# Masks of attention tiles: two of a group's sixteen on GpSimd, one on VectorE, thirteen on TensorE

## The reference, cut to what matters

```python
q, k, v = (proj(Wq), proj(Wk), proj(Wv))              # 8 sequences, 16 heads, 512 tokens, 16 features
scores = jnp.einsum('bhsd,bhtd->bhst', q, k) * scale
scores = jnp.where(mask[None, None, :, :], -jnp.inf, scores)
attn = jax.nn.softmax(scores, axis=-1)
out = jnp.einsum('bhst,bhtd->bhsd', attn, v)
```

## Time and profile before

| | |
|---|---|
| median of three runs | 1219.8 us (1218.94 to 1219.91) |
| the profiled execution: its time | 1216.96 us |
| the profiled execution: its span | 1215.2 us |
| TensorE busy | 1139.1 us (94%) |
| VectorE busy | 824.7 us (68%) |
| ScalarE busy | 736.8 us (61%) |
| GpSimd busy | 534.0 us (44%) |
| mean granted TensorE clock | 0.983 of 2.4 GHz |

### The profile page before, as it was taken

The page is one execution under the profiler, slowest core; times in us unless marked ns, Lnnn a source line. Parts: engine busy times, 40 slices in busy tenths (PEclk is TensorE's granted clock), DMA queues, the critical chain, the costliest instruction groups (busy, mean ns, idle before and its releaser), DMA issues.

```text
span 1215.2 us, 23411 instructions
## 1 busy us (share of the span) xinstructions
PE 1139.1 (94%) x7533; PEld 769.8 (63%) x7590; DVE 824.7 (68%) x2331; ACT 736.8 (61%) x1632; POOL 534.0 (44%) x805
## 2 busy tenths in 40 slices
PE   6899999999989989998888899999999999999978
PEld 3333433434434334343322899999999999999968
DVE  4688879687897887877772444464555655667647
ACT  2266666575666666666546566566666666666645
POOL 7234225484673765747535347546222222323210
PEclk9899999999999999999889899999999999999999
DMA  6654635647448455483543658975655774833536
GB/s 194 185 192 153 200 114 178 200 166 196 136 162 258 140 165 159 153 251 104 177 173 118 228 152 283 340 220 114 189 152 133 233 233 121 277 61 67 157 87 208
DMA packets 101456, 213.52 MB, mean 176 GB/s; under 512 B 10885, under 2 KB 71181, under 8 KB 92886
## 3 DMA queue, kind: packets, MB, share of 16 engines
q1 hardware_dynamic: 87030, 193.34, 49.3%
q0 software_dynamic: 14304, 18.69, 8.3%
HBM read 239.15 MB, written 74.29 MB: 258 GB/s over the span
## 4 chain that ended last, share of the span: by engine, by line
PE 67%; POOL 11%; issue 5%; DVE 5%; DMA 4%; ACT 3%; SPq 3%; another core or an unknown queue 0%; DVEq 0%; POOLq 0%; ACTq 0%
PE bank L1023 36%; PE bank L1123 6%; PE bank L1092 5%; PE bank L1104 5%; PE bank L1108 4%; POOL routed L1882 3%; DMA w_parts<-in_W 2%; PE bank L1068 2%; PE bank L1141 2%; DVE junk L1551 1%; ACT pt L1284 1%; POOL ssq L793 1%; SPq L879 1%; PE bank L1181 1%; PE bank L1076 1%
## 5 line engine op out<-in xcount | busy, mean ns | idle before, releaser
L1284 ACT ACTIVATE pt<-bank 128x512 f32<-128x512 f32 x512 | 300.5, 595 | 178.2 <-PE bank L1108 125.2
L1551 DVE CUSTOM_DVE_ANT_0 junk<-bank,mneg 128x512 bf16<-128x512 f32 x512 | 336.1, 684 | 100.5 <-PE bank L1092 99.5
L1023 PE MATMUL bank<-hid,w 128*128 128x256 f32 x1872 | 241.9, 286 | 4.2 <-DVE hid L1699 4.2
L1699 DVE TENSOR_TENSOR hid<-full,hid 128x256 fp32r<-128x256 f32 x312 | 138.4, 449 | 148.0 <-ACT full L1358 145.8
L1892 POOL DMA_INDIRECT x<-yout,rows x78 | 122.6, 1572 | 263.8 <-ACT yout L1363 235.5
L1023 PEld LDWEIGHTS bank<-hid,w 128*128 128x128 f32 x1872 | 228.6, 191 | 5.2 <-issue 3.1
L1353 ACT ACTIVATE hid<-bank,biases 128x256 fp32r<-128x256 f32 x312 | 150.7, 483 | 103.5 <-PE bank L1023 102.7
L1358 ACT ACTIVATE full<-bank,biases 128x256 f32<-128x256 f32 x312 | 150.3, 482 | 0.0
L1108 PE MATMUL bank<-mneg,identb 128*128 128x512 bf16 x391 | 149.9, 383 | 0.0
L1023 PE MATMUL bank<-rowsT,w 128*128 128x256 f32 x936 | 122.8, 285 | 6.1 <-DMA w<-split_weights 5.2
L1123 PE MATMUL bank<-pt,vaug 128*17 128x512 f32 x1024 | 124.3, 604 | 1.9 <-ACT pt L1284 0.7
(11 more groups left out here) (184 smaller groups left out, 1492.3 us busy)
## 6 DMA issues: line engine op xcount, KB each, us to landing
w<-split_weights SPq DMA_DIRECT2D x80, 1024.0 KB
w<-split_weights SPq DMA_DIRECT2D x40, 2048.0 KB
split_weights<-w_parts SPq DMA_DIRECT2D x64, 512.0 KB, 4.2
w_parts<-in_W SPq DMA_DIRECT2D x64, 256.0 KB, 4.5
split_parts<-parts SPq DMA_DIRECT2D x28, 384.0 KB, 2.6
rows<-routed SPq DMA_DIRECT2D x39, 258.0 KB, 3.6
stacks<-split_parts SPq DMA_DIRECT2D x36, 256.0 KB, 7.4
qst<-split_parts SPq DMA_DIRECT2D x24, 256.0 KB, 7.6
```

The costliest lines, as they stand in the source:

```text
L1023: product = T.matmul(ps, w[p], x[q], start=(k == 0 and n == 0), stop=(k == len(weights) - 1 and n == 2))
L1284: A.activation(pt[n % len(pt)][:, :], bank[3 + n % 2][:, :], ACT.Exp, scale=float(D) ** -0.5).then_inc(exped.sem, 1)
L1551: V.tensor_tensor_reduce(junk[n % 2][:, :], bank[n % 3][:, :], mneg[:, 0, st, :], 1.0, FLOOR, ALU.add, ALU.max, rowmax[gi % 2][:, hh, st:s ...
L1699: V.tensor_tensor(lo, h[:, :], hi.bitcast(F32), ALU.subtract).then_inc(hidden_low.sem, 1)
```

## The change

- `attention_order` writes a clear step only for kt 2 of head 0. For kt 0 it writes two new steps "blank", for heads 0 and 2, at k = 0, n = 1 and n = 3.
- A blank step is GpSimd's: it waits for the exponential, reads the buffer `pt` as 32-bit integers and multiplies them by `keep`, a new 128 x 512 tile of integer ones and zeros, in place. `keep` holds the mask of keys 0 to 127 and is made once, by one more VectorE instruction at the start.
- Col steps of kt 0 of heads 0 and 2 have no product with `mneg`. So thirteen of sixteen col steps of a group have it, and fourteen had it before. The weigh step of kt 0 waits for the second blank in place of the clear.
- `squared` is one buffer, and each square waits for the one before it. The two `mrow` buffers become partitions 0 to 7 and 32 to 39 of one buffer.

```diff
@@ -60,6 +60,9 @@
 MATRIX_PAUSE = 4
+BLANKED = 0, 2
...
@@ -277,7 +280,9 @@
                     out.append(("col", i - 2, k, n))
-                    if k % 2 == 0 and n == 2:
+                    if k == 0 and n % 2:
+                        out.append(("blank", i - 2, n - 1))
+                    if k == 2 and n == 2:
                         out.append(("clear", i - 2, k, 0))
...
@@ -486,7 +491,7 @@
     wo = lasting("wo", [P, NG // 2, E])
-    squared = [lasting(f"squared{i}", [P, E], BF16) for i in range(2)]
+    squared = lasting("squared", [P, E], BF16)
     gain_shift = [lasting(f"gain_shift{i}", [P, 2 * E]) for i in range(2)]
...
@@ -521,13 +526,15 @@
     mneg = sb("mneg", [P, 2, ST, S], BF16)
+    keep = sb("keep", [P, S], I32)
     qst = [stacks0[:, 0], sb("qst1", [P, H, S], BF16)]
     m2 = [sb(f"m2_{i}", [P, ST, P], BF16) for i in range(2)]
-    mrow = [sb(f"mrow{i}", [GH * SHIFTS, S], BF16) for i in range(2)]
+    mrows = sb("mrows", [2 * 32, S], BF16)
+    mrow = [mrows[32 * i:32 * i + GH * SHIFTS, :] for i in range(2)]
     pt = [sb(f"pt{i}", [P, S]) for i in range(12)]
...
@@ -631,6 +638,7 @@
     cleared = signal("cleared", of("clear"))
+    blanked = signal("blanked", of("blank"))
     normal = Count(sem("normal"), [(at, 3 + at[0] % 2) for at in of("normalise")])
...
@@ -700,6 +708,7 @@
     CONSTANTS = 23
+    MASKS = 5
     CHANGED = 2 * NTILES
...
@@ -909,7 +918,7 @@
                     sp.wait_ge(*last_col(b - 2))
-                start(qst[b % 2][KQ:KQ + SHIFTS, gi % NG * GH:(gi % NG + 1) * GH, :], mrow[gi % 2][:, :]).then_inc(dma_mrow[gi % 2], 16)
+                start(qst[b % 2][KQ:KQ + SHIFTS, gi % NG * GH:(gi % NG + 1) * GH, :], mrow[gi % 2]).then_inc(dma_mrow[gi % 2], 16)
             elif name == "pads":
...
@@ -1100,11 +1109,11 @@
                 pe.wait_ge(constants_made, CONSTANTS)
-                limit = (gi, kt, hh) in cleared.value
+                limit = (gi, kt, hh) in cleared.value or kt == 0 and (gi, hh) in blanked.value
                 product = T.matmul(ps[:, :], kst[b % 2][0:KQ + SHIFTS, h, kt * P:(kt + 1) * P], qst[b % 2][0:KQ + SHIFTS, h, :],
                 if not limit:
-                    pe.wait_ge(masks_made, 4)
+                    pe.wait_ge(masks_made, MASKS)
                     product = T.matmul(ps[:, :], identb[:, :], mneg[:, 1, kt, :], start=False, stop=True)
...
@@ -1116,7 +1125,9 @@
                 pe.wait_ge(*exped.at((gi, kt - kt % 2 + 1, GH - 1)))
-                if kt % 2 == 0:
+                if kt == 0:
+                    pe.wait_ge(*blanked.at((gi, BLANKED[-1])))
+                elif kt == 2:
                     pe.wait_ge(*cleared.at((gi, kt, 0)))
...
@@ -1232,9 +1243,9 @@
         def square(sums, src, n):
-            if n >= 2:
-                act.wait_ge(squares.sem, n - 1)
-            A.activation(squared[n % 2][:, :], src, ACT.Square, accum_out=sums).then_inc(squares.sem, 1)
+            if n:
+                act.wait_ge(squares.sem, n)
+            A.activation(squared[:, :], src, ACT.Square, accum_out=sums).then_inc(squares.sem, 1)
...
@@ -1274,7 +1285,7 @@
                     act.wait_ge(dma_mrow[gi % 2], 16 * (gi // 2))
-                A.activation(mrow[gi % 2][:, :], ps[0:GH * SHIFTS, :], ACT.Copy).then_inc(max_rows.sem, 1)
+                A.activation(mrow[gi % 2], ps[0:GH * SHIFTS, :], ACT.Copy).then_inc(max_rows.sem, 1)
             elif name == "col":
...
@@ -1523,6 +1534,7 @@
                 V.tensor_scalar(mneg[:, 1], mask8[:, 1], MASKED, None, ALU.mult).then_inc(masks_made, 1)
+                V.tensor_scalar(keep[:, :], mask8[:, 1, 0], 0.0, None, ALU.is_equal).then_inc(masks_made, 1)
             elif name == "prepare":
...
@@ -1780,6 +1792,12 @@
                 assert made[0] == CONSTANTS, made
+            elif name == "blank":
+                gi, hh = at
+                bits = pt[col_place[gi, 0, hh] % len(pt)][:, :].bitcast(I32)
+                pool.wait_ge(*exped.at((gi, 0, hh)))
+                pool.wait_ge(masks_made, MASKS)
+                G.tensor_tensor(bits, bits, keep[:, :], ALU.mult).then_inc(blanked.sem, 1)
             elif name == "split_chunk":
...
```

More of the change, by code:

```diff
@@ L1292, in scalar_program @@
                 else:
-                    act.wait_ge(masks_made, 4)
+                    act.wait_ge(masks_made, MASKS)
                 A.activation(osb[:, st, :], ps[:, 0:E], ACT.Copy).then_inc(o_ready.sem, 1)
@@ L1545, in vector_program @@
                 dve.wait_ge(*row_scored.at((gi, hh, st)))
-                dve.wait_ge(masks_made, 4)
+                dve.wait_ge(masks_made, MASKS)
                 if n >= 2:
```

## The result

The changed kernel takes 1231.1 us (median of four executions, 1229.99 to 1234.61) against 1219.4 us for the kernel before beside it: a ratio of 1.0107 (95% interval 1.0083 to 1.0132), +13.1 us by the ratio and +11.7 us by the medians. The forecast was slower, at 1226.8 us, with a range of 1215 to 1238. The direction held and the time lies in the range; the size did not hold: 7.0 us were forecast, and the interval begins at +10.1. Its profiled execution took 1231.05 us, with a span of 1229.3 us (before: 1215.2 us).

The account below looks back on a forecast made before the run. Much of each sequence was held bound by GpSimd, then SP and its transfers; elsewhere mostly by TensorE. Terms 8.5 + 1.7 + 2.2 - 5.4 = +7.0 us on 1219.8 gave 1226.8 us, range 1215 to 1238.

Parts of the forecast that it names:

- The view of the bound: From 244.69 to 294.40, 50 us of a sequence's some 80, GpSimd, then SP and its transfers set the time.
- The blank's price: One integer product of 512 elements on GpSimd was taken at 1.3 us, with bounds of 1.2 and 2.6.
- The rival of a slow product: Blanks take some 1.9 us or more on GpSimd: 1237 us, or 1249 at 2.6 us each; chance 0.10.
- my estimate of 1.9 us: A blank's time by the skill's two-times-slower rule on the removed clears' 0.97 us mean; would give 1237 us.
- The root late by 2.0 us in a sequence: Sequences 1 to 4: blanks ahead of GpSimd's inverse root delay it 2.0 us, less in the third.
- In sequence 5: One blank ahead of the root, two behind it: 1.3 + 0.4 = 1.7 us of cost.
- Hits of scalings, 0.4 us: A blank behind the root holds one of VectorE's four scalings: between 0 and 1.3 us, taken as 0.4.
- The saving, 5.4 us: Outside the chain, 18 groups each save 0.3 us through the dropped product and clear.
- The 0.08 us for VectorE: Part of each of 18 groups' saving, credited to VectorE's shorter queue without the clear.
- The gap of 1.16 us behind the long clear: TensorE's wait at 281.15, once a sequence, would go, but was counted as nothing because it lies in the chain.
- The end, 2.2 us: Last group: blanks finish at 658.3, holding a weigh step and so the first fetch of the experts by 2.2 us.
- The rival "no change": Half of the delay is absorbed, 6 us of cost against 5.4 saved: 1217.4 to 1222.2 us; chance 0.13.

Follow-up runs that it names:

- e7: Changed kernel with ten extra TensorE products ahead of the row step waiting for the late scaling, in groups 14, 18, 22, 26: +12.3 us over the kernel before (1.0101).
- e6: Changed kernel with groups 30 and 31 masked as in the kernel before: +10.0 us over the kernel before (ratio 1.0082).
- the layout's trace: Profile of the kernel before with only the change's buffers (one `squared`, joined `mrows`, `keep`), all old masks, no blanks: +0.6 us over the kernel before (1.0005).
- r1: The changed kernel itself once more, on another call's chip: +12.6 us over the kernel before (ratio 1.0103).
- r3: Changed kernel without its 64 multiplications, those tiles left unmasked, for timing alone; a repeat on another chip: -4.5 us against the kernel before (0.9963).
- r4: Kernel before in the new buffer layout, all old masks, plus 64 GpSimd multiplications on `keep` that no weigh step awaits; a repeat: +6.3 us (1.0052).
- e9: Changed kernel with blanks of half the size, only queries 0 to 255 multiplied, for timing alone: -1.1 us against the kernel before (0.9991).

## Why the prediction was right, and where its size was off

**The view of the bound held.** The chain GpSimd, root, scaling, sums, SP, transfer of the maxima sets the time, and e7 and e6 show its last link best: what TensorE gets back ahead of it, it waits away at the transfer.

**The blank's price held**: 1.3 us taken, 1298 ns measured. An integer product takes what the sum of two tiles takes (1290 ns in the earlier trace rows). The rival of a slow product fell. The Trainium skill, GPSIMD Engine Reference, section "Engine selection", puts GpSimd at about two times slower with two inputs; the trace agrees when the undisturbed clear is taken (0.69 us in the layout's trace, so 1.8 times), while my estimate of 1.9 us from it took the clear's mean, which has waits in it.

**The root late by 2.0 us in a sequence: the mechanism held, the size was too big.** The scaling waits 2.95, 2.71, 2.72 and 2.70 us in sequences 1 to 4 (0.95, 0.94, 1.31 and 0.94 before), so 2.0, 1.8, 1.4 and 1.8 more; 2.0, and 0.9 in the third, was the forecast. That these numbers met is in part luck. By the table of the root's end it came only 1.8, 1.2, 0.1 and 1.2 us later than before. The rest of the wait is VectorE's: its clear, 1.03 us beside `xin` before, now begins just before `xin` (269.05 against 269.09) and isn't held, so VectorE is at the scaling earlier. Two blanks also pushed less than their 2.6 us less 0.96: the pair of `parts` took 2.72 us before and 1.16 and 1.17 with a blank between them.

In sequence 5 the scaling waits 0.2 us more and not 1.3 to 1.7; the delay came out ahead of it. I had placed the blanks of that group behind the scatters and overlooked the one ahead of the ranks. Its rows in r1, where groups 25 to 29 lose 3.4 us (2.1 in the first execution, 0.8 with the layout alone): GpSimd stands 2.63 us for the exponential of the blank, with the ranks behind it in the queue, and VectorE later waits behind the second blank, 1.97 us (1.05 in the layout's trace). Only a part of the 2.63 is lost: in the layout's trace GpSimd stands 3.50 us there for the ranks themselves. The ranks' first step comes 0.4 us later against the end of the chunk, and the wait of 1.97 adds 0.9:

```profile
561.28 1.30 POOL L1800 TENSOR_TENSOR pt<-pt,keep 128x512 int32<-128x512 int32 x1 [2.63 <-ACT pt L1295]
562.52 0.19 POOL L802 COPY run<-run 128x8 f32<-128x8 f32 x1
...
569.16 0.19 DVE L1409 TENSOR_REDUCE gs<-gt 128x4 f32<-128x32 f32 x1 [1.97 <-POOL gt L802]
```

**Hits of scalings, 0.4 us: the size of a term, but of another instruction.** No scaling of sequences 1 to 4 was held: they take 0.79, 0.87, 0.48 and 0.48 us, as before. The blank of 277.86 held the split's CAST between them, 0.66 us for 0.20, and the four scalings are done 5.01 us after the first began, where it was 4.56. In sequence 5 they take 6.37 us for 4.83: the first is held (1.46 us), and the split (1.23).

**The saving, 5.4 us: held** by the times of r3 (4.5), and so did 0.22 us a group: the row of groups 4 to 10 reads -1.4 for six of them. The 0.08 us for VectorE were never seen. The gap of 1.16 us behind the long clear did go: the second quarter of groups 14, 18, 22 and 26 is 1.3 us shorter, in the changed kernel and in r3. The forecast counted nothing, since the chain would take it, and r3 bears that out: with the four groups behind them they are together only 1.4 us shorter than before. In the changed kernel TensorE was late by the new gap, and the chain had less to take. r4, which keeps the clear at 2.46 to 2.48 us, is 1.3 us shorter only in groups 14 and 26, where TensorE came late behind a fall of the clock (weigh steps of 3.41 and 3.45 us).

**The end, 2.2 us: too small.** It measured 3.3 us by the traces, and by e6 all of it belongs to the last two groups. By the times e6 wins 2.6 us, less than its uncertainty. The wait is 2.97 us (2.2 forecast), and behind it the weigh step runs at half the clock, 1.7 us longer, which the forecast did not have. No transfer hides this one in the way e7 found for the sequences; of the two together 3.3 us reach the first expert product.

**What was missing altogether: group 0, +3 us.** I had looked for VectorE instructions with two inputs in SBUF only beside the root. The split of the maxima is of that kind and is met there as well (above), but most of all in the first group, since GpSimd has nothing else to do there and runs both blanks the moment the exponentials come. The row shows that an instruction of 16 elements waits for one of 512 to end, 0.23 against 1.30 us. The Trainium skill, SBUF — State Buffer, section "Who interferes with whom", says so: a VectorE instruction with two SBUF inputs contends with a GpSimd one that reads SBUF, and the one that comes second is blocked for the whole of the first. The trace agrees for the split. The CAST ahead of it, with one input, was held too (0.20 to 0.96 us); the same section counts casts among the operations that can contend. Subtraction and CAST together lose 1.8 us of the 3; behind them TensorE's clock is at 0.50 for the 3.2 us shown above, which I take for the rest.

By places the sum would then read: group 0 +3; the sequences about +10, of which the rows show the root later than in r3 (5.3 us), the split in four sequences (4 x 0.45 = 1.8), and ranks and scalings in sequence 5 (1.3 + 1.5); the end +3.3; savings -4.5; in all +12. Measured were +11.7 and +12.6. The 10 us are an estimate from waits, and no run took each of them out alone. They agree with 8.5 + 1.7 in the forecast, though not term by term: its root was to be 6.9 us later over four sequences, where 4.2 were measured against before and 5.3 against r3, and its fifth sequence lost elsewhere. What failed in the prediction is the list of places (group 0 at nothing where 3 us were lost, the end at 2.2 where it was 3.3), and not its mechanism: its costs of 12.4 us were 17. The rival "no change" described a reserve that covers half; e9 shows that there is a reserve, the chunk's wait, which takes up 0.73 us a blank nearly whole, and that 1.27 us lies above it.

## What to carry to other kernels

Price work added to an engine's queue by what is awaited behind it, place by place, and list all places before summing: here one pair of 1.3 us instructions in the very first group cost as much as a whole sequence's. Don't read an engine's wait as the lateness of what it waits for: the waiting engine may have come earlier, or both may hang on a third (r3, e9 and r4 have the same wait with roots a microsecond apart). Half the dose is a cheap experiment to learn whether a delay is covered by a reserve. And a stretch at half the clock is worth chasing only where no later wait takes the time back, which extra work in the gap tells at once.

## What the runs showed of the hardware

- GpSimd's integer product of two tiles, 128 x 512, takes 1.27 us and 128 x 256 takes 0.73; with one tile for both inputs the larger takes 1.04.
- VectorE's 16-element subtraction took 1.30 us beside a blank and 0.23 without it, and a 16-element CAST 0.96 and 0.20.
- TensorE was granted 2.4 GHz ahead of a gap of 2.76 us and 1.2 GHz for the 6.5 us behind it; behind a gap of 0.55 us, with ten products ahead of it, it stayed at 2.4 GHz. Behind gaps of 2.5 us and more it fell in nine of twelve cases, behind gaps of 1.2 to 1.7 us in four of twelve (r3, e9 and r4): the same gap can go either way.
- VectorE's clear of 128 x 512, 0.68 us alone, took 2.25 us where it met `xin` on GpSimd.
- One chip ran the kernel before in 1238.7 us, where it took 1218.2 to 1219.4 elsewhere, and four other kernels' traces from it have stalls of TensorE of 1.3 to 2.2 us at places where before's and the layout's have none; most of its extra time lies in the experts' stage and later.
